# A Trainium2 attention and mixture-of-experts kernel: output in two DRAM tensors, and each block's scatter-add in two halves of the columns

## What is computed

```
x = x + xattn(layernorm(x), ctx)
x = x + ffn(layernorm(x))        # rows are the 2048 (batch, channel) pairs, D = 512

h      = rmsnorm(...)            # t = 2048 rows
topv, topi = top_k(softmax(h @ router_w), 2)        # 8 experts, 2 for each row
moe    = sum over the 2 experts of  w * (silu(h @ w_gate[e]) * (h @ w_up[e])) @ w_down[e]
sh     = silu(h @ sw_gate) * (h @ sw_up) @ sw_down  # a shared expert for all rows
out    = x + moe + sh
```

## Time and profile before

| | |
|---|---|
| median of 3 runs | 884.27 us (884.0 to 884.33) |
| the profiled execution | 882.7 us |
| its span, first to last instruction | 880.9 us |
| mean granted clock of TensorE over the span | 0.977 of full speed |
| PE busy | 827.0 us (94%) |
| DVE busy | 518.6 us (59%) |
| ACT busy | 401.1 us (46%) |
| POOL busy | 223.1 us (25%) |
| moved by DMA | 110.45 MB, 125 GB/s in the mean |

### The profile page before, as it was taken

How to read it: one execution, slowest core, us unless ns; L and a number is a source line. 1 busy time by engine, 2 the same in 40 slices (tenths; PEclk the granted TensorE clock), 3 DMA queues, 4 the chain that set the end, 5 groups by cost and what they waited for, 6 DMA issues and landing times. The chain is left out here.

```text
span 880.9 us, 11075 instructions
## 1 busy us (share of the span) xinstructions
PE 827.0 (94%) x3641; PEld 376.0 (43%) x3641; DVE 518.6 (59%) x1043; ACT 401.1 (46%) x751; POOL 223.1 (25%) x206
## 2 busy tenths in 40 slices
PE   6889999999999999999999999999999999999991
PEld 2334333334334333343343355443545555555550
DVE  5686788787777777777778755568532222222220
ACT  1104666656667666666676663110323333323220
POOL 4203013213232132132200111000114444444431
PEclk9879999999999999999999999999999999999996
DMA  8876365546546655565551232941625555455542
GB/s 272 187 195 192 88 136 136 134 90 157 127 109 137 148 136 121 103 160 124 115 108 29 84 92 74 389 148 48 249 63 96 90 92 93 90 95 94 95 84 36
DMA packets 47017, 110.45 MB, mean 125 GB/s; under 512 B 11684, under 2 KB 12708, under 8 KB 42724
## 3 DMA queue, kind: packets, MB, share of 16 engines
q1 hardware_dynamic: 35548, 80.23, 36.0%
q0 software_dynamic: 11328, 29.37, 16.2%
q10 hardware_dynamic: 88, 0.16, 0.1%
HBM read 68.44 MB, written 41.16 MB: 124 GB/s over the span
## 5 line engine op out<-in xcount | busy, mean ns | idle before, releaser
L850 DVE TENSOR_REDUCE negmax<-front_ps 128x1 f32<-128x512 f32 x512 | 323.8, 682 | 108.7 <-PE front_ps L702 108.3
L637 ACT ACTIVATE probs<-st_ps 128x512 f32<-128x512 f32 x512 | 280.1, 600 | 187.0 <-PE st_ps L736 186.6
L1289 PE MATMUL big_ps<-w_gu,attn 128*128 x312 | 140.4, 593 | 0.8 <-ACT attn L1138 0.8
L1099 POOL DMA_INDIRECT out<-x_sb,row_i x39 | 61.7, 1583 | 136.0 <-DMA out<-x_sb,row_i 108.5
L736 PE MATMUL st_ps<-stacks 50*128 50x512 f32 x256 | 78.7, 496 | 7.6 <-ACT probs L637 4.4
L1483 DVE TENSOR_TENSOR zeros<-attn,big_ps 128x256 f32<-128x256 f32 x39 | 16.4, 421 | 116.4 <-ACT attn L1157 116.4
L1289 PEld LDWEIGHTS big_ps<-w_gu,attn 128*128 128x128 f32 x312 | 56.2, 190 | 57.0 <-issue 57.0
L736 PE MATMUL st_ps<-q_stack,k_stack 50*128 50x512 f32 x256 | 74.8, 492 | 3.8 <-ACT probs L637 2.7
L702 PE MATMUL front_ps<-stacks 48*128 48x512 f32 x256 | 71.3, 450 | 5.5 <-DMA stacks<-parts_dram 3.0
L374 POOL TENSOR_TENSOR attn<-attn,recip 128x512 f32<-128x512 f32 x15 | 19.2, 1279 | 207.8 <-DMA recip<-rec_dram 207.8
L673 PE MATMUL proj_ps<-early,w_t 128*128 128x512 f32 x128 | 67.2, 647 | 4.7 <-ACT early L590 2.5
(11 more groups left out here) (167 smaller groups left out, 902.0 us busy)
## 6 DMA issues: line engine op xcount, KB each, us to landing
parts_dram<-early SPq DMA_DIRECT2D x32, 512.0 KB, 4.7
stacks<-parts_dram SPq DMA_DIRECT2D x32, 256.0 KB, 5.6
w_gu<-in_gate_up SPq DMA_DIRECT2D x8, 1024.0 KB, 14.4
x_sb<-in_x SPq DMA_DIRECT2D x8, 512.0 KB, 7.4
early<-in_ctx POOLq DMA_DIRECT2D x8, 512.0 KB, 8.2
stacks<-parts_dram SPq DMA_DIRECT2D x32, 128.0 KB, 6.3
k_stack<-parts_dram SPq DMA_DIRECT2D x16, 256.0 KB, 5.0
q_stack<-parts_dram SPq DMA_DIRECT2D x16, 256.0 KB, 5.8
```

Of the source, the lines that this page charges most:

```text
L637: nc.scalar.activation(probs[:, k % 2, u % GH, :], score_bank(UNITS * s + u), ACT.Exp, scale=SCALE).then_inc(exp_done, 1)
L850: nc.vector.tensor_reduce(negmax[:, n % 2, c:c + 1], smax_bank(UNITS * n + u), AX_X, ALU.max, negate=True).then_inc(max_done, 1)
L1099: nc.gpsimd.indirect_dma_start(out_rows, bass.IndirectOffsetOnAxis(ap=row_i[:, k:k + 1], axis=0), y_sb[:, k % RING, :], None, compute_op=A ...
L1289: mm = nc.tensor.matmul(gu_ps[:, :], h_t[:, k % 2, a, :], w_gu[:, bass.ds(expert, 1), a, :], start=(a == 0), stop=(a == DT - 1))
```

## The change

The output is two DRAM tensors of 256 columns instead of one of 512 (YCUT = 2, DY = 256), put together on the host. Each base store is two DMAs, one per tensor, from the two halves of the tile's columns. Each block's scatter-add is two: the first half of the columns of y_sb into the first tensor, the second half into the second, each with a counter of its own (y_added[0], y_added[1]), so that a half waits for the same half of the block before. Both stand ahead of the gather. The counts of the other waits follow, and clearing the spare rows of the output takes two DMAs.

```diff
 def xattn_ffn_kernel(nc, x, ctxt, wqkv_t, wo_t, bias_cols, rms_w, router_t, gate_up, down,
-                     sh_gate_up, sh_down, out):
+                     sh_gate_up, sh_down, *outs):
...
-    out_rows = out
-    out_t = out[0:NTILE * P, :].rearrange("(n p) t -> n p t", p=P)
+    out_t = [out[0:NTILE * P, :].rearrange("(n p) t -> n p t", p=P) for out in outs]
...
-                        nc.gpsimd.dma_start(out_rows[NTILE * P:, :], zeros[:, :]).then_inc(dump_cleared, 16)
-                pool.wait_ge(dump_cleared, 16 * 2)
+                        for i in range(YCUT):
+                            nc.gpsimd.dma_start(outs[i][NTILE * P:, :], zeros[:, 0:DY]).then_inc(dump_cleared, 16)
+                pool.wait_ge(dump_cleared, 16 * (1 + YCUT))
...
-        y_added = sem("y_added")
+        y_added = [sem(f"y_added{i}") for i in range(YCUT)]
...
                 def store_base(t):
                     sp.wait_ge(shared_added, t + 1)
-                    sp.dma_start(out_t[t], x_sb[:, t, :]).then_inc(base_first if t < 2 * RING else base_rest, 16)
+                    for i in range(YCUT):
+                        sp.dma_start(out_t[i][t], x_sb[:, t, DY * i:DY * (i + 1)]
+                                     ).then_inc(base_first if t < 2 * RING else base_rest, 16)
...
-                sp.wait_ge(base_first, 16 * 2 * RING)
-                sp.wait_ge(base_rest, 16 * (NTILE - 2 * RING))
+                sp.wait_ge(base_first, 16 * YCUT * 2 * RING)
+                sp.wait_ge(base_rest, 16 * YCUT * (NTILE - 2 * RING))
...
-                pool.wait_ge(base_first, 16 * 2 * RING)
+                pool.wait_ge(base_first, 16 * YCUT * 2 * RING)
                 for k in range(RING):
                     gather(k)
-                pool.wait_ge(dump_cleared, 16 * 2)
-                pool.wait_ge(base_rest, 16 * (NTILE - 2 * RING))
+                pool.wait_ge(dump_cleared, 16 * (1 + YCUT))
+                pool.wait_ge(base_rest, 16 * YCUT * (NTILE - 2 * RING))
                 for k in range(BLOCKS):
                     pool.wait_ge(y_copied, k + 1)
-                    if k >= 1:
-                        pool.wait_ge(y_added, 16 * k)
-                    nc.gpsimd.indirect_dma_start(
-                        out_rows, bass.IndirectOffsetOnAxis(ap=row_i[:, k:k + 1], axis=0),
-                        y_sb[:, k % RING, :], None, compute_op=ALU.add).then_inc(y_added, 16)
+                    for i in range(YCUT):
+                        if k >= 1:
+                            pool.wait_ge(y_added[i], 16 * k)
+                        nc.gpsimd.indirect_dma_start(
+                            outs[i], bass.IndirectOffsetOnAxis(ap=row_i[:, k:k + 1], axis=0),
+                            y_sb[:, k % RING, DY * i:DY * (i + 1)], None, compute_op=ALU.add).then_inc(y_added[i], 16)
                     if k + RING < BLOCKS:
                         gather(k + RING)
-                pool.wait_ge(y_added, 16 * BLOCKS)
+                for i in range(YCUT):
+                    pool.wait_ge(y_added[i], 16 * BLOCKS)
...
                     if k >= RING:
-                        act.wait_ge(y_added, 16 * (k - RING + 1))
+                        for i in range(YCUT):
+                            act.wait_ge(y_added[i], 16 * (k - RING + 1))
...
-                act.wait_ge(base_first, 16 * 2 * RING)
+                act.wait_ge(base_first, 16 * YCUT * 2 * RING)
```

More of the change, by code:

```diff
@@ L49 @@
 STORED = 8
+YCUT = 2
+DY = D // YCUT
 def xattn_ffn_kernel(nc, x, ctxt, wqkv_t, wo_t, bias_cols, rms_w, router_t, gate_up, down,
-                     sh_gate_up, sh_down, out):
+                     sh_gate_up, sh_down, *outs):
     x_t = x.rearrange("b (o p) t -> b p o t", p=P)
@@ L1531 @@
         args.append(nc.dram_tensor(f"in_{name}", a.shape, mybir.dt.from_np(a.dtype), kind="ExternalInput").ap())
-    args.append(nc.dram_tensor("out_0", (B * C + P, T), F32, kind="ExternalOutput").ap())
+    for i in range(YCUT):
+        args.append(nc.dram_tensor(f"out_{i}", (B * C + P, DY), F32, kind="ExternalOutput").ap())
     xattn_ffn_kernel(nc, *args)
     r = run_bass_kernel_spmd(nc, [arrays], core_ids=[0])
-    return r.results[0]["out_0"][:B * C].reshape(B, C, T)
+    return np.concatenate([r.results[0][f"out_{i}"][:B * C] for i in range(YCUT)], axis=-1).reshape(B, C, T)
```

## The result

| | before | changed |
|---|---|---|
| first series, median (lowest to highest) | 884.3 us (881.95 to 888.48), 6 runs | 874.8 us (871.2 to 877.65), 6 runs |
| second series, median (lowest to highest) | 884.19 us (881.87 to 892.61), 11 runs | 873.83 us (872.32 to 877.48), 6 runs |
| profiled execution | 882.7 us | 871.2 us |
| its span | 880.9 us | 869.5 us |

The ratio is 0.9888 (95% interval 0.9859 to 0.9916), in the second series 0.9887 (0.9860 to 0.9915). The kernel is 9.5 us faster in the first series.

What follows compares the result with a forecast made beforehand. The prediction took the chain of scatter-add landings, 5.6 us a block beside TensorE's 5.49, as the bound. It summed -1.4 us (rate) and -1.4 us (end) to -2.8 us, 881.5 us by the median; range 878.0 to 890.0.

Steps and rivals of the forecast that it cites:

- The bound, and what the change does to it: Expert stage: scatter chain of 5.6 us a block holds back TensorE's 5.49; halved, its link is 4.8, no longer a bound.
- The base stores and the added waits: Ahead of and around the scatters: smaller, doubled base stores and extra waits cost nothing, with 9 and 4.6 us of cover.
- The rate: Expert blocks: 5.56 us a block instead of 5.60, over 36 blocks a gain of 1.4 us.
- from a copy's end to its scatter it takes 0.86 us at least: Expert stage: shortest time from a weighted copy's end to its scatter's start, 0.86 us, used in the two-block sum.
- The gather's landing: Expert stage, gather behind two scatters: 3.5 us until TensorE gets the rows, against 4.2 before; bounds 3.1 and 4.2.
- the loop: Copy, scatters, gather and TensorE's wait for its rows, closing over two blocks: 10.85 us against TensorE's 10.98.
- The end: Blocks 37 and 38: the last half lands at 872.2 against 873.7 us, 1.4 us less.
- My lower bound of 3.7: Landing of a half scatter: bounds 3.7 and 4.8 us, 4.0 taken; the lower end saves at most 1.03 us.
- The Trainium skill's fit: Landing of a half: a DMA as about 2.0 us plus bytes at 436 GB/s, saving 0.30 us, not 0.8.
- What lies behind the last landing: From the last scatter's landing to the end of the span: taken to have no record and to stay unchanged.
- The gather as the bound: TensorE's wait for gathered rows: gather still needs 4.2 us, 5.83 a block, +6.9 us, 891.2 us; chance 0.25.
- That POOL goes by bytes: POOL's scatter records: 0.79 us a half instead of 1.58, TensorE bounds at 5.50 a block, 876.8 us; chance 0.08.

Runs made afterwards that it cites:

- run 5: The kernel before, with the gather of block k+4 issued ahead of the wait for block k's weighted copy, one scatter earlier: 883.6 us.
- run 2: The changed kernel, but each half's scatter waits for the landing of the half before it, in one chain of 78 halves: 1004.63 us.
- run 3: The changed kernel with four cuts instead of two: four output tensors of 128 columns, four chains: 1007.51 us.
- run 1: The kernel before, unchanged, profiled a second time: 882.88 us.
- run 6: The changed kernel with the gather of block k+4 issued ahead of the wait for block k's weighted copy: 872.18 us.
- run 4: The changed kernel without the second half's scatter-adds, so columns 256 to 511 get the base alone: 877.7 us.
- runs 8 and 13 to 15: More gathers after the last scatter: 10 on the changed kernel, 914.57 us; 10, 20 and 30 on the kernel before, 920.9, 956.81 and 993.22 us.
- run 7: The kernel before with 39 more gathers, one by one, after its last scatter has landed: 1019.78 us with the extra gathers' time.
- run 9: The changed kernel, unchanged, timed again beside the kernel before and profiled a second time: 873.83 us, ratio 0.9887.

## Why the prediction was wrong

**The bound, and what the change does to it: right.** The chain of scatters was the bound; run 5 takes TensorE's waits away and gains nothing, run 2 puts one chain back, of 78 links, and loses all and 120 us more. Halves in chains of their own make TensorE the bound. POOL's record does not go by bytes (run 3). The base stores and the added waits cost nothing that shows: the first copy comes no later than the starts vary (run 1).

**The rate: a term mis-sized.** I had 5.56 us a block, a gain of 1.4 us; measured are 5.52 and 5.51, against the first profile's 5.60 a gain of 36 x 0.08 = 2.9 us. The step that failed in it is "from a copy's end to its scatter it takes 0.86 us at least". In the changed kernel it is 674.14 - (673.18 + 0.69) = 0.27 us. I had read it from the first block, the only one before in which the chain does not come last, and the first block is a case of its own: it takes 652.42 - (650.54 + 0.69) = 1.19 us in the changed kernel too. Nor is the copy quicker to wake POOL than a landing: run 2 has 0.27 us behind a landing too, where it is the only wait ahead of the scatter, and 0.75 where it is the second. The place of the wait in POOL's program goes with the number; why, no run shows. The gather's landing, 3.5 in my sum, is 3.4. So the loop is 2.73 + 0.27 + 3.74 + 3.4 = 10.1 us against 10.98, with a slack of 0.9 us where I had 0.13, and late gathers cost little but for the one of run 6.

**The end: mis-sized.** The last landing comes 8.0 us after the last copy's end (865.9 against 857.27 + 0.69), where I had 8.6 (872.2 against 863.6) and the kernel before 10.1. A half lands after 3.7 to 3.8 us, not 4.0, and the end has two in a row. My lower bound of 3.7, all of the time on the rings halved, was the better value: the whole's 4.8 less 1.03 is 3.8. The Trainium skill's fit (page "DMA: Bandwidth & Descriptors", the anatomy of one SWDGE DMA) would give 0.30 us for 128 KB; the runs here show 1.0, so for an accumulating scatter it does not hold. With the fixed part of about 2.0 us that the Trainium skill gives there, a scatter of 64 KB would take an estimated 2.15 us. Run 3 shows 3.3, and a line through the three sizes leaves an estimated 2.8 for no bytes at all, of which POOL's own record is 1.55; so the fixed part is larger here too.

**What lies behind the last landing: the step that failed and put the time outside the range.** "What follows up to the end of the span has no record and stays." It has a record, in the sequencer's rows, and it did not stay: POOL's DRAIN went from 6.76 to 3.05 us, 3.7 us, more than either other part. Had it stayed, the median would be 874.8 + 3.7 = 878.5, just inside the range. That is no merit of halves. Half the bytes in the same number of transfers have the old length (run 4), and ten transfers more move it by 0.8 us or by a tooth of the sawtooth (runs 8 and 13 to 15). Why it is 3.05 us in the changed kernel stays open: 39 more transfers on the kernel before gave 4.07 (run 7).

The sum: 2.8 forecast, 1.5 more in the rate, 0.6 at the end, 3.7 in the DRAIN make 8.6 us, where the medians say 9.5 and 10.4. The profile that I summed against had the shortest stage of the seven of its kind (run 9), 1.3 us under their middle value of 221.0; that covers the rest.

**The rivals.** The gather as the bound did not come: it is behind both halves, but lands 0.8 us sooner, as the rows of the rings said. The rule that halves serialize (the Trainium skill, same page, rules for kernel authors) agrees with the rings' time: from 700 to 800 us they are busy for 0.60 with both halves and 0.39 with one (run 4), so the second comes on top (0.21 x 5.5 = 1.2 us a block), and the whole's 0.52 did not shrink. Yet most of a half's 3.8 us to landing is not that time, and the two chains hide it beside each other; run 2 shows what halves strictly one after the other cost. That POOL goes by bytes would have given 876.8, near the measured time, by a mechanism that is not there.

## What to carry to other kernels

Where a chain of dependent accumulating DMAs bounds a stage, cut the data, not the order: independent pieces in chains of their own hide each other's landing time, of which bytes make the smaller part (3.3 us are left at a quarter of them), as long as the issuing engine has room for a cost that does not shrink with the bytes (here 1.9 us for each scatter of 128 rows with its gap, so two pieces in 5.5 us and not four). Close the loop of every prefetch that stands behind the added work, and take each wake-up from a row in which the same wait, at the same place in the program, comes last. And look at the end of the program in the sequencer's rows, also where the engines are idle: a DRAIN can be as large as the effect one is after, and change with it for another reason.

## What was not expected of the hardware

- POOL's DRAIN at the end takes 0.94 to 6.76 us in these kernels. It came out the same to the nanosecond when the same program was profiled again (6.763 us before, 3.050 changed), was the same for half the bytes (run 4), rises by 0.05 to 0.08 us per transfer, and falls back at some counts. A DRAIN in the middle has a record that also spans the transfers in flight (9.8 and 11.4 us).
- An indirect DMA of 128 rows has the same record on POOL for rows of 2048, 1024 and 512 bytes: 1.58, 1.55 to 1.57 and 1.55 us with the add. A gather takes 0.99 to 1.02.
- A scatter starts 0.27 us after what it waited for, copy (changed kernel) or landing (run 2), where that is the first wait ahead of it, 0.75 to 0.8 us where it is the second, and 0.86 or 1.19 us after the copy in the first block, where two other waits stand ahead of that for the copy.
